# A graph layer's edge counts in tiles of two 14-destination groups, and biases summed on TensorE

## The reference, cut to what matters

```python
edge_index = jnp.stack([src, dst])
xn = _layernorm(x, axis=-1)
x = x + _L0_gnn_ref(xn, edge_index, edge_type_3, ...) + _L0_mix_ref(xn[None], ...)[0]
x = x + _L0_ffn_ref(_layernorm(x, axis=-1)[None], ...)[0]
```

```python
qkv = x @ W_qkv + b_qkv
...
kv = jnp.einsum('bhnd,bhne->bhde', kf, v)
y_num = jnp.einsum('bhnd,bhde->bhne', qf, kv)
y_den = jnp.maximum(jnp.einsum('bhnd,bhd->bhn', qf, kf.sum(axis=2))[..., None], EPS)
y = y_num / y_den
```

## Time and profile before

| | us |
|---|---|
| median of three executions (1670.88, 1674.98, 1675.16) | 1674.98 |
| the profiled execution | 1673.72 |
| its span on the core | 1672.0 |
| stage K's turns | 74.9 to 123.6 |
| stage V | 123.6 to 221.8 |
| stage Q from its second block on | 290.9 to 367.3 (first block from 252.5) |
| stage Y | 372.9 to 427.5 |

### The profile page before, as it was taken

One profiled execution on the slowest core, in us unless ns is written; L12 is line 12 of the kernel. 1 busy time (PEld: TensorE's weight loads), 2 busy tenths in 40 slices (PEclk: granted clock), 3 DMA queues, 4 the chain that ended last, 5 costly groups with the idle time before them and its releaser, 6 DMA issues.

```text
span 1672.0 us, 34410 instructions
## 1 busy us (share of the span) xinstructions
PE 1574.0 (94%) x10567; PEld 1139.5 (68%) x10568; DVE 1313.5 (79%) x2633; ACT 809.4 (48%) x1074; POOL 144.4 (9%) x280
## 2 busy tenths in 40 slices
PE   5899998988999999999999999989999999999987
PEld 4566675666556666699999999976555555555544
DVE  7699968989489999288898998972774577777795
ACT  6331115552235664378888888962222233333352
POOL 3000000000100000000000000000000143333340
PEclk9999998999999999999999999989999999999998
DMA  6111115520456663540132033023766521101212
GB/s 208 37 60 59 60 48 175 165 81 29 133 190 217 201 199 115 177 131 31 62 94 62 31 115 118 14 89 98 210 204 187 203 79 56 53 3 56 89 38 93
DMA packets 129294, 178.54 MB, mean 107 GB/s; under 512 B 15509, under 2 KB 100606, under 8 KB 129202
## 3 DMA queue, kind: packets, MB, share of 16 engines
q1 hardware_dynamic: 129202, 177.38, 33.7%
HBM read 120.47 MB, written 56.88 MB: 106 GB/s over the span
## 4 chain that ended last, share of the span: by engine, by line
PE 71%; issue 15%; DVE 7%; ACT 2%; DMA 2%; DVEq 1%; POOL 0%; SPq 0%; POOLq 0%; ACTq 0%
PE ps L2219 23%; PE ps L2173 14%; PE ps L2279 7%; PE ps L2278 7%; PE ps L1993 4%; PE ps L2084 3%; PE ps L1980 2%; PE ps L1981 2%; PE ps L1982 2%; DVE oh_q L1472 1%; PE ps L2290 1%; PE ps L2156 1%; DVE oh_p L1473 1%; PE ps L2036 1%; ACT q_m L1092 1%
## 5 line engine op out<-in xcount | busy, mean ns | idle before, releaser
L2219 PE MATMUL ps<-xrh,pf 128*128 (+1 forms) x2400 | 399.0, 329 | 4.8 <-DVE pf L1758 4.8
L2219 PEld LDWEIGHTS ps<-xrh,pf 128*128 128x128 f32 x2400 | 392.5, 190 | 11.2 <-issue 9.0
L1980 PE MATMUL ps<-w_hi,xt_hi 128*128 128x384 f16 x600 | 197.6, 329 | 10.0 <-DVE ev_t L1507 3.4
L2278 PE MATMUL ps<-x,ph 128*128 (+1 forms) x600 | 195.2, 325 | 11.8 <-POOL pl L991 11.8
L1758 DVE SCALAR_TENSOR_TENSOR pf<-vb,CT 128x1260 f32<-128x1260 f32 x118 | 172.8, 1468 | 33.6 <-PE ps L2219 33.6
L1981 PE MATMUL ps<-w_lo,xt_hi 128*128 128x384 f16 x600 | 197.4, 329 | 0.0
L1982 PE MATMUL ps<-w_hi,xt_lo 128*128 128x384 f16 x600 | 197.2, 329 | 0.0
L2279 PE MATMUL ps<-x,ph 128*128 (+1 forms) x600 | 196.5, 328 | 0.0
L1472 DVE TENSOR_SCALAR oh_q<-pat,codeT,neg_w 125x630 f16<-125x630 uint16 x420 | 185.0, 441 | 13.8 <-PE ps L1993 7.7
L1754 DVE SCALAR_TENSOR_TENSOR vb<-vb,tb 128x1260 f32<-128x1260 f32 x118 | 170.0, 1466 | 12.7 <-ACT vb L1226 11.8
L1666 DVE CUSTOM_DVE_ANT_0 tt_junk<-kbc,mb 126x1260 bf16<-126x1260 f32 x120 | 169.1, 1466 | 11.7 <-issue 11.7
(11 more groups left out here) (266 smaller groups left out, 2359.1 us busy)
## 6 DMA issues: line engine op xcount, KB each, us to landing
qbc<-tq_d SPq DMA_DIRECT2D x12, 1260.0 KB, 6.5
wst<-in_L_gnn_W SPq DMA_DIRECT2D x60, 192.0 KB, 3.2
xr_d<-ev SPq DMA_DIRECT2D x60, 192.0 KB, 2.0
x_d<-ev SPq DMA_DIRECT2D x60, 192.0 KB, 2.4
mb_d<-mb SPq DMA_DIRECT2D x30, 310.1 KB
mb<-mb_d SPq DMA_DIRECT2D x30, 310.1 KB
xrh<-xr_d SPq DMA_DIRECT2D x3, 2880.0 KB, 15.5
x<-x_d SPq DMA_DIRECT2D x2, 3840.0 KB, 18.1
```

What stands on the lines that cost most here:

```text
L1980: pe.matmul(ps[:, bank, 0:CW], a_hi, hi[:, k, :], start=(k == 0), stop=False)
L2219: mm = pe.matmul(out[b], pf[j][:, b * DB:b * DB + P], x, start=(first and b % 2 == 0), stop=False, skip_group_check=True)
L2278: pe.matmul(ps[:, bank, 0:CW], p, cols(off, off + CW), start=start, stop=False, skip_group_check=True)
```

## The change

**Counts.** The window's group shrinks from 21 to 14 destinations (`oh_q` 420 columns), and a window holds two groups, each with its own bank and five tiles: ten tiles a turn in units of 4, 3 and 3. One matmul of 420 columns serves a tile. There are 45 such windows in place of 60: 450 tiles in place of 420, 450 matmuls of 420 columns in place of 840 of 315, and two opening matmuls of 2 columns per window. Stages K, V and S keep their 33 windows; stage Q has two per block (at k = 3 and behind k = 5) in place of three, stage Y none in place of nine.

**Codes.** The offset leaves VectorE: POOL (`codes_of`) reads the window's two words, writes each turn's ten codes plus offset (`cw`) and ten slots (`sw`) into a ring of four, and VectorE's one-hots compare with one scalar each. POOL's loop for windows 0 to 32 stands ahead of its chain for stage Q, the loop for 33 to 44 behind that chain.

**Table.** 96 groups in place of 64 windows; it goes to DRAM in two writes (96 elements of 2 bytes, 48 of 4) in place of one (64 of 4).

**Biases of k and v.** POOL splits them into three bf16 rows in the layer norm's stage, a DRAM round trip lays them out as `krow`, and one matmul of 3 rows by 384 columns per product adds them in TensorE's sum (40 products). `k_sum` goes: ScalarE and `k_part` read the bank itself, which is free only behind `k_part`. VectorE's add for `V` goes: ScalarE copies, and frees the bank. A load of 768 KB that had spread the biases goes.

```diff
-WN = 21
+WN = 14
...
-TF = 4
-TM = 3
-TG = TF + TM
+TT = 5
+TG = 2 * TT
+UNITS = ((0, 4), (4, 7), (7, 10))
+RR = 4
...
-        QW = 3
+        QW = 2
...
+            def codes_of(w):
+                tiles = pool.value_load(tabrow[0:1, ds(w, 1)], ...)
+                count, first = window(pool, w)
...
+                with pool.Fori(0, count) as jj:
+                    n1 = pool.snap(first + jj + 1)
+                    o = pool.snap(n1 & (RR - 1), min_val=0, max_val=RR - 1)
+                    pool.wait_ge(cw_free, n1)
+                    for u in range(2):
...
+                        pool.tensor_tensor(cw[0:ET, ds(o, 1), TT * u:TT * u + TT]..., codeT[0:ET, ds(t, TT)],
+                                           neg_w[0:ET, ds(2 * w + u, 1)].to_broadcast([ET, TT]), ALU.add)
+                        last = pool.tensor_copy(sw[0:ET, ds(o, 1), TT * u:TT * u + TT]..., sloT[0:ET, ds(t, TT)])
+                    last.then_inc(cw_done, 1)
...
+            pool.wait_ge(tab_io, 48)
+            with pool.Fori(0, W_Q) as w:
+                codes_of(w)
             pool.wait_ge(qk_ready, 64)
             pool.tensor_scalar(qkn[:, :, :, :], qkn[:, :, :, :], SPLIT, None, ALU.mult).then_inc(qk_ready, 1)
...
+            with pool.Fori(W_Q, NWP) as w:
+                codes_of(w)
...
+            def one_hots(count, first):
                 with dve.Fori(0, count) as jj:
                     n1 = dve.snap(first + jj + 1)
+                    o = dve.snap(n1 & (RR - 1), min_val=0, max_val=RR - 1)
+                    dve.wait_ge(cw_done, n1)
+                    for i in range(len(UNITS)):
+                        dve.wait_ge(oh_free[i], n1)
+                        for k in range(*UNITS[i]):
+                            a = dve.tensor_scalar(oh_q[0:ET, k, :], pat[0:ET, :], cw[...], None, ALU.is_equal)
+                            b = dve.tensor_scalar(oh_p[0:ET, k, :], iota_l[0:ET, :], sw[...], None, ALU.is_equal)
+                        b.then_inc(oh_rdy[i], 1)
+                    a.then_inc(cw_free, 1)
...
-            def k_sum(c, n, j):
...
-                dve.tensor_tensor(ev_t[j][:, :], ps[:, 6 + j, 0:CW], bk_bc[:, c * CW:(c + 1) * CW], ALU.add).then_inc(g_free, 1)
...
-                    if k in (1, 3, 4)[:QW - 1]:
-                        count_part(wa + (1, 3, 4).index(k) + 1)
+                    if k == 2:
+                        count_part(wa + 1)
...
+                if bias:
+                    pe.matmul(ps[:, bank, 0:CW], kone[:, :], krow[:, c * CW:(c + 1) * CW], start=True, stop=False)
...
-                        if k in (2, 4, 5)[:QW - 1]:
-                            u = (2, 4, 5).index(k)
-                            count_window(wa + u, 6, *of_w[u])
+                        if k == 3:
+                            count_window(wa, 6, *of_w[0])
...
-                for w in block_windows(i):
-                    count_window(w, 6, *window(pe, w)[1:])
```

More of the change, by code:

```diff
@@ L61 @@
 QN = NB * KN
[L62 to L63 removed]
+NTAB = 96
 GN = GW // WN
@@ L657, in _ @@
                 for u in range(QW):
-                    for t in ((0, 1), (2, 3), (4,), (5,))[u] if QW == 4 else ((0, 1), (2, 3), (4, 5))[u]:
+                    for t in range(3 * u, 3 * u + 3):
                         wq_load(6 * q + t + 6)
@@ L781, in _ @@
             sp.wait_ge(kq_st, 32)
-            for u in range(2):
+            for u in range(WU):
                 for r in range(R):
@@ L1517, in _ @@
             tables(1)
-            dve.wait_ge(bias_in, 32)
             for p in range(NB // 2):
-                for j in range(2):
-                    k_sum(0, 2 * p + j, j)
                 if p < 3:
@@ L1585, in query_block @@
                                              ALU.add, ALU.max).then_inc(q_out, 1)
-                count_part(wa + QW)
+                if more:
+                    count_part(wa + QW)
             count_part(W_Q)
@@ L1960, in table_sums @@
                 pe.wait_ge(e_row, 6)
-                pe.wait_ge(e_const, 1)
-                pe.matmul(ps[0:NTAB, 0, 0:1], ltri[:, :], tab[:, 1:2], start=True, stop=True).then_inc(e_tr, 1)
+                pe.wait_ge(e_const, 2)
+                for c in range(2):
+                    last = pe.matmul(ps[0:NTAB // 2, 0, c:c + 1], ltri[:, c, :], tab[:, 1:2], start=(c == 0), stop=(c == 1), skip_group_check=True)
+                last.then_inc(e_tr, 1)
             for p in range(NB // 2):
@@ L1973, in _, with product @@
                         last.then_inc(tr_done, 1)
-            def product(c, t_hi, t_lo, i, bank):
+            def product(c, t_hi, t_lo, i, bank, bias=False):
                 hi, lo = w_hi[c % 2], w_lo[c % 2]
+                if bias:
+                    pe.matmul(ps[:, bank, 0:CW], kone[:, :], krow[:, c * CW:(c + 1) * CW], start=True, stop=False)
                 for k in range(K6):
                     a_hi, a_lo = t_hi[:, k, ds(i * P, P)], t_lo[:, k, ds(i * P, P)]
-                    pe.matmul(ps[:, bank, 0:CW], a_hi, hi[:, k, :], start=(k == 0), stop=False)
+                    pe.matmul(ps[:, bank, 0:CW], a_hi, hi[:, k, :], start=(k == 0 and not bias), stop=False)
                     pe.matmul(ps[:, bank, 0:CW], a_hi, lo[:, k, :], start=False, stop=False)
@@ L2024, in _ @@
                         w = W_K + (c - 1) * NB + 2 * ii + j
-                        _, count, first = window(pe, w)
-                        pe.wait_ge(g_free, n + 1)
-                        product(c, xt_hi, xt_lo, 2 * ii + j, 6 + j).then_inc(g_done, 1)
+                        count, first = window(pe, w)
+                        if c == 1:
+                            pe.wait_ge(kv_out, n + 1)
+                        else:
+                            pe.wait_ge(g_free, n + 1)
+                        product(c, xt_hi, xt_lo, 2 * ii + j, 6 + j, True).then_inc(g_done, 1)
                         count_window(w, 2 * j, count, first)
```

298 lines of the change are left out of this document (153 added, 145 removed).

## The result

| | us |
|---|---|
| before, four executions | 1670.88 to 1675.16, median 1674.97 |
| changed kernel, four executions | 1693.88, 1696.68, 1705.06, 1707.47, median 1700.87 |
| ratio, with its 95% interval | 1.016 [1.011, 1.021] |
| profiled execution and its span | 1707.47, 1705.8 |

A forecast was written before the change was run, and what follows sets the result against it. It took PE's rate to bound K and V, a chain through PE and DVE Q, and DVE's one-hots Y. Terms 4 + 5 + 6.2 + 2.4 + 2.8 - 2.5 - 5.7 = +12.2 on 1673.72 gave 1686 us, range 1667 to 1699.

The forecast's parts named there:

- Where the counts begin: Chain ahead of stage K's first turn: four lengthenings make it start 5 us later, bounds +2 and +12.
- term (b): Table's write to DRAM: 144 small elements in place of 64 add 1.5 us, between nothing and 7.5.
- Rival 3: Table's write goes by its number of elements: +6 on the forecast, 1692 us; chance 0.10.
- Term (a): Six products ahead of the table: bias matmuls (1.0) and banks held through `k_part`, together +1.5 us, bounds 1 and 2.
- Term (c): Before the first one-hots: POOL reads two words and computes codes, net +1.5 us.
- Term (d): First one-hots ahead of stage K: ten tiles take 4.1 us for 3.63, +0.5.
- K, V and S: Turns of K and V grow 0.13 to 4.99 us, thirty give about +4, bounds 0 and +8; S adds 0.
- The start of Q: First `wt_lo` waits for POOL's chain, then codes (2.0) and one-hots (4.1): +6.2 us, bounds +4.8 and +7.5.
- Query blocks: Stage Q: wait near 2 us at k = 2 makes five blocks +2.4; lower clock behind it +2.8.
- Y: Stage Y without one-hots: entry -2.5 us, nine blocks -5.7 with two in three at the lower clock; bounds -17 and +1.
- Rival 1: Clock stays at 1.00 in Y and Q, Y's gain pays for the rest: +0.5, 1674 us; chance 0.28.
- Rival 2: POOL and DVE hinder each other in K, V and Q: +21, 1707 us, half of it 1696; chance 0.10.

The follow-up runs named there:

- run with split waits: Changed kernel with a wait between the table's two writes, so each write's time shows; 1700.61 us.
- the two order runs: Changed kernel, first `wt_lo` of a query block ahead of its first one-hots: 1686.99 us; also fourth `wt_lo` ahead of second one-hots, ScalarE's eviction later: 1682.39 us.
- The fillers: Changed kernel plus ten unread matmuls (five in later blocks) in TensorE's idle stretch behind each stage Y block; 1697.88 us, stage 43.9 for 53.5.

## Why the prediction was wrong

The direction held, the size did not: 26 for a forecast of 12.2, and outside the range. By its own steps, with the profiled execution's 33.8:

- **Where the counts begin, forecast +5, measured +15.0.** This is the step that failed. Its term (b), the table's write, was put at +1.5 "near the lower end" and took +7.4, the upper end of its bounds. The argument against the upper end, that a write costing by its elements "would leave nothing for the transfer itself", was no measurement, and a write near 13 had been named as a sign of being wrong. The run with split waits puts 12.6 on the 96 elements of 2 bytes, and the run with one write gives 11.4 back. I argued over the number alone; that the elements were now half as long and on 96 partitions in place of 64 was not weighed, and which of these counts is not shown. Rival 3 had price and place right, at a chance of 0.10, but its price per element is refuted by three runs. Term (a) was +3.5 and not +1.5: six bias matmuls cost 0.36 each and not 0.16, and the held bank cost a wait of 2.24 and 3.0 at the low clock behind it, where 0.5 had been put. Some of it is not on top: before the change the first product had lost some 1.7 at a clock of 0.51, and PE had stood 1.43 waiting for DVE ahead of the column sums. Term (c) was +3.5 and not +1.5: POOL's first code came 6.14 behind the issue of the table's read, where DVE's first one-hot had come 3.85 behind it, and its own one-hot follows 1.2 later. Term (d), forecast +0.5, was +0.3, and the second write's issue takes the rest.
- **K, V and S, forecast +4, measured +9.2.** A turn is +0.27, not +0.13, and thirty are 8.1; the rest is the longer gaps at three places and the clock. (From the first turn to the last window it is 172.1 before, and 179.2 to 181.5 in six profiles with the new turns; the one told here is near the top.) The ten matmuls' columns were right (1.79); the bias matmul takes 0.265 where 0.16 was put, and the gap ahead of it went from 0.03 to 0.10. I had priced a matmul by its columns alone. That the add removed from DVE pays nothing in V was forecast, and PE without a gap inside the turns bears it out. Why the bias matmul costs more than its columns stays open; neither the loop nor the window is it.
- **The start of Q, forecast +6.2, measured +7.5.** Right, by the mechanism stated; from the chain's end to the first one-hot it took 3.2 where 2.0 were put. The run with the codes ahead takes all of it back.
- **Query blocks, forecast +5.2, measured +8.5.** The wait at k = 2 was there, 2.41. The first block gave 1.1 of it, the second 1.7, three of the other four 1.0 to 1.1 each. The remaining one gave 2.6 (365.73 to 387.38), at a granted clock of 0.92: that is the second price of the wait, some 1.5 where 2.8 had been put. A block is 20.2 for a forecast of 19.6. I had the first wait, and not the one that stands behind it; the two order runs show both. That more could be had back (17.6) than the change had added shows that DVE had slack here, which its order did not use.
- **Y, forecast -8.2, measured -7.1.** Right, with the clock as the reason: blocks of 4.47 and of 5.6 to 6.3, where 4.45 and 5.9 had been put. The fillers show that the clock is the cause. That six of nine were long, just as forecast, is partly luck: in the ten profiles with this stage unchanged three to seven were. The rule of the Trainium skill that the prediction set beside this (TensorE: Matmul & The Clock Gate, section A second HAM failure mode: psum-queue depth-cycling) agrees in kind: the clock swung, 1.00 in three blocks and 0.50 to 0.73 in the six others. That it would fall in every block was my reading of that rule, and the trace is against it.
- **Rival 1** fell with the clock at 0.72 in Y. **Rival 2** is half true: POOL slows beside DVE (last section), but the one-hots did not slow beside POOL. `oh_q` had a mean of 322 ns, tiles 0.40 each for a forecast of 0.41. That its 1707 is the time of the profiled execution is chance.

The 13.6 between executions is a part that the sum did not have: the mean clock granted differs from one to the next, and only the profiled one, the slowest of the four, shows in which stretches it fell. So the steps add up to 33.8, and the medians differ by 26.

## What to carry to other kernels

Price a small DMA write only from a row of the same shape (bytes of an element, elements and partitions of one transfer); where no row has that shape, let the forecast reach the dear end. Where narrow columns can be packed into one write, that can pay: here it gave 11.4 back for two small products. When work leaves an engine that was the bound, ask what its order now waits for: here 2.6 us a query block lay in the order of two small `wt_lo` and one eviction, and in stage Y the freed time came back as idle time that cost TensorE its clock. A ring that another engine fills is only as early as that engine's program order: its first turn after a pause must stand ahead of whatever that engine does in the pause.

## What the runs showed of the hardware

- A write of 96 elements of 2 bytes from 96 partitions to DRAM took 12.6, one of 48 elements of 4 bytes 3.2, of 64 of 4 bytes 6.0, of 48 of 8 bytes 2.3 to 2.7. Why the first is so dear is not shown: neither the bytes of an element, nor the elements or partitions of a transfer, nor the spacing in DRAM was varied by itself.
- A matmul with three rows of weights and 384 columns took 0.265 to the next start, where one with 128 rows takes 0.162, behind a matmul of 2 columns as behind one of 384. The gap ahead of it was 0.1, and a product of eighteen matmuls went from 2.93 to 3.29 with it.
- POOL's operations stretch beside DVE. Timelines of POOL and DVE in the changed kernel, in the first and second query block:

```profile
281.02 0.51 POOL L955 TENSOR_TENSOR cw<-codeT,neg_w  x1 [2.37 <-issue]
305.46 2.55 DVE L1542 TENSOR_TENSOR w_lo<-wst,w_hi 128x2304 f16<-128x2304 f32 x1
306.03 4.64 POOL L955 TENSOR_TENSOR cw<-codeT,neg_w  x1 [9.21 <-DVE oh_q L1531]
307.93 2.69 DVE L1600 SCALAR_TENSOR_TENSOR wt_lo<-wt,wt_hi 128x768 f16<-128x768 f32 x3
```

An operation of 0.20 takes 0.51 beside one-hots, and 4.64 beside `w_lo` and `wt_lo`, which read two operands from SBUF. It began 0.6 behind `w_lo` and ended at 310.67, together with the third `wt_lo` (310.62). The Trainium skill (SBUF — State Buffer, section Who interferes with whom) says that a DVE instruction with two SBUF inputs contends with a GpSimd instruction that reads SBUF; this row agrees. The ring of four covers it: DVE's one-hots waited 23.6 in all for codes, and the two starts are 12.76 and 10.80 of that.
